# A linear-attention and feed-forward block on one core: K sums in two fp16 parts, a moved projection, a later load and another order in the first tile

## What is computed

```
q, k, v = heads(xn @ Wq), heads(xn @ Wk), heads(xn @ Wv)     # 16 heads of 64
q, k = elu(q) + 1, elu(k) + 1
k_sum = k.sum(over rows)
z = einsum(q, k_sum) + 1e-6
kv = einsum("bhnd,bhne->bhde", k, v)
out = (q @ kv / z) @ Wo + bo                                  # x = x + out
h = square(relu(xn2 @ W_fc.T));  y = h @ W_proj.T
x = x + (count of spikes of y over 5 steps) / 5
```

## Time and profile before

| what | value |
|---|---|
| median of 3 runs | 1036.33 us (1036.07 to 1036.6) |
| profiled execution, its own time | 1036.43 us |
| its span | 1034.6 us |
| PE busy | 1026.2 us |
| DVE, ACT, POOL busy | 873.8, 737.3, 654.7 us |
| TensorE clock granted | 1.00 of full speed |

### The profile page before, as it was taken

One profiled execution on the slowest core, in us unless ns is written; L12 is line 12 of the kernel. 1 busy time (PEld: TensorE's weight loads), 2 busy tenths in 40 slices (PEclk: granted clock), 3 DMA queues, 4 the chain that ended last, 5 costly groups with the idle time before them and its releaser, 6 DMA issues.

```text
span 1034.6 us, 19797 instructions
## 1 busy us (share of the span) xinstructions
PE 1026.2 (99%) x6999; PEld 653.0 (63%) x6999; DVE 873.8 (84%) x1871; ACT 737.3 (71%) x1216; POOL 654.7 (63%) x410
## 2 busy tenths in 40 slices
PE   8999999999999999999999999999999999999998
PEld 4444444444444467777777767777777777777887
DVE  7899887898888699888888888888888888888875
ACT  8888677778768758676666767676767676676664
POOL 1444434455345488777778676878777777777835
PEclk9999999999999999999999999999999999999999
DMA  4546553225323545454454454455444444544441
GB/s 132 148 127 145 121 122 88 77 63 122 87 69 82 122 76 113 93 107 99 96 128 108 82 105 95 105 106 98 97 108 108 93 103 107 108 93 93 78 80 45
DMA packets 265284, 104.24 MB, mean 101 GB/s; under 512 B 219360, under 2 KB 262624, under 8 KB 265184
## 3 DMA queue, kind: packets, MB, share of 16 engines
q1 hardware_dynamic: 265040, 102.90, 44.7%
q10 hardware_dynamic: 144, 0.07, 0.0%
HBM read 33.69 MB, written 16.79 MB: 49 GB/s over the span
## 4 chain that ended last, share of the span: by engine, by line
PE 97%; DMA 1%; DVE 1%; ACT 1%; issue 0%; ACTq 0%; DVEq 0%
PE proj L619 31%; PE acc L784 16%; PE acc L820 16%; PE acc L662 15%; PE acc L759 8%; PE acc L768 4%; PE acc L761 4%; PE proj L696 1%; PE proj L684 1%; DMA xT<-xnat 1%; ACT feat L879 0%; PE acc L633 0%; PE proj L673 0%; DMA x_t<-in_L_attn_x_dram 0%; ACT feat L875 0%
## 5 line engine op out<-in xcount | busy, mean ns | idle before, releaser
L875 ACT ACTIVATE feat<-proj 128x1024 f32<-128x1024 f32 x123 | 125.7, 1022 | 193.7 <-PE proj L619 193.7
L1555 POOL TENSOR_TENSOR qT<-qT,feat 128x1024 f32<-128x1024 f32 x60 | 142.4, 2373 | 174.8 <-DVE xnat L1186 151.3
L1590 POOL TENSOR_TENSOR h<-h_f,h 128x512 f16<-128x512 f32 x128 | 148.8, 1183 | 159.2 <-ACT h L1052 159.2
L784 PE MATMUL acc<-xn2T,wfcT 128*128 128x256 f16 x1536 | 178.0, 273 | 0.0
L820 PE MATMUL acc<-wpT,h 128*128 128x256 f16 (+1 forms) x1560 | 177.9, 271 | 0.1
L662 PE MATMUL acc<-feat,xnat 128*128 128x512 f16 x768 | 176.2, 379 | 0.0
L619 PE MATMUL proj<-wk,xT 128*128 128x512 f16 x756 | 173.3, 379 | 0.7 <-DMA xT<-xnat 0.4
L784 PEld LDWEIGHTS acc<-xn2T,wfcT 128*128 128x128 f16 x1536 | 150.3, 98 | 28.9
L1561 POOL TENSOR_TENSOR feat<-feat,rz 128x1024 f32<-128x1024 f32 x60 | 165.8, 2764 | 2.8 <-DVE rz L1293 2.8
L619 PE MATMUL proj<-wq,xT 128*128 128x512 f16 x720 | 165.2, 379 | 0.0
L820 PEld LDWEIGHTS acc<-wpT,h 128*128 128x128 f16 x1560 | 150.6, 98 | 22.7 <-issue 0.3
(11 more groups left out here) (106 smaller groups left out, 1317.9 us busy)
## 6 DMA issues: line engine op xcount, KB each, us to landing
x_t<-in_L_attn_x_dram SPq DMA_DIRECT2D x128, 128.0 KB, 2.3
xT_spill<-xT SPq DMA_DIRECT2D x64, 128.0 KB, 2.0
out_dram<-out_t SPq DMA_DIRECT2D x63, 128.0 KB, 2.1
xT<-xT_spill SPq DMA_DIRECT2D x60, 128.0 KB, 2.3
ks_all<-ks_rows SPq DMA_DIRECT2D x4, 512.0 KB, 4.5
qT<-feat SPq DMA_TRANSPOSE x120, 3.1
m_all<-in_L_attn_Wk_dram SPq DMA_DIRECT2D x4, 256.0 KB, 4.3
xT<-xnat SPq DMA_TRANSPOSE x64, 2.4
```

The costliest lines, as they stand in the source:

```text
L784: mm = pe.matmul(acc[:, 2 + g % 2, f % 2 * 2 * P:(f % 2 + 1) * 2 * P], wfcT[:, left, f * C2 + c2, :], xn2T[:, pair % 4, right * C2 + c2, : ...
L1555: pool.tensor_tensor(kacc[:, b % 2, :], kacc[:, b % 2, :], k_feat(n), ALU.add).then_inc(k_added, 1)
L1590: pool.tensor_tensor(lo, h_f[:, k % 4, :], hi, ALU.subtract).then_inc(h_lo, 1)
```

## The change

Four things. The K sums of batches 0 to 2 are split into fp16 parts, high by ACT (`ks_hi_part`, two rounds ahead of kv) and low by DVE (`ks_lo_part`, one round ahead), both scaled by 1/16, into slot 3 of `qT`; `ks_job` then runs eight fp16 matmuls of 256 columns instead of four in fp32. The two M guests of batch 2 go from rounds 54 and 56 of the K stage to steps 15 and 18 of `LATE`. `load_ks` comes one round later. `first_k_tile` completes one half of the columns before it begins the other. The order of `JOBS`, by which semaphores count, follows.

```diff
+        ks16 = qT[:, 3, :, :].rearrange("p (h k) n -> p h (k n)", h=2)
+        ones16 = sb("ones16", [P, 32], F16)
...
-        JOBS = [job for b in range(B) for job in in_order(b)]
+        JOBS = [("kv", 0, 0), *m_jobs(0), ("kv", 1, 0), *m_jobs(1), ("kv", 2, 0), ("kv", 3, 0), *m_jobs(2), *m_jobs(3)]
...
-                  52: ("kv", 2, 0), 54: ("m", 2, 0), 56: ("m", 2, 1)}
+                  52: ("kv", 2, 0)}
...
-        LATE = {7: ("kv", B - 1, 0), 26: ("m", B - 1, 0), 29: ("m", B - 1, 1)}
+        LATE = {7: ("kv", B - 1, 0), 15: ("m", 2, 0), 18: ("m", 2, 1), 26: ("m", B - 1, 0), 29: ("m", B - 1, 1)}
...
+                if n == 3:
+                    sp.wait_ge(ks_full, B - 1)
...
-                if n - 5 in GUESTS and GUESTS[n - 5][0] == "kv":
-                    load_ks(GUESTS[n - 5][1])
+                if n - 6 in GUESTS and GUESTS[n - 6][0] == "kv":
+                    load_ks(GUESTS[n - 6][1])
...
-                for right, lefts, ready in ((HI, (HI, LO), w_hi), (LO, (HI,), w_split)):
-                    for half in range(2):
-                        cols = slice(half * HALF, (half + 1) * HALF)
+                for half in range(2):
+                    cols = slice(half * HALF, (half + 1) * HALF)
+                    for right, lefts, ready in ((HI, (HI, LO), w_hi), (LO, (HI,), w_split)):
...
-                        if right == LO:
-                            mm.then_inc(k_proj if half else k_half_proj, 1)
+                    mm.then_inc(k_proj if half else k_half_proj, 1)
...
+                if b < B - 1:
+                    pe.wait_ge(ks_lo, b + 1)
+                    groups = ks16.rearrange("p h (j a r) -> p h a j r", a=4, r=32)
+                    for part in (HI, LO):
+                        for a in range(4):
+                            mm = pe.matmul(ks_bank(b)[32 * a:32 * a + 32, :], ones16[:, :], groups[:, part, a],
+                                           start=(part == HI), stop=(part == LO), skip_group_check=True)
...
+            def ks_hi_part(b):
+                act.wait_ge(k_added, BT * (b + 1))
+                wait_past(act, ks_full, b)
+                act.activation(ks16[:, HI, :], kacc[:, b % 2, :], ACT.Copy, scale=KS_SHARE).then_inc(ks_hi, 1)
...
+                if n + 2 in GUESTS and GUESTS[n + 2][0] == "kv":
+                    ks_hi_part(GUESTS[n + 2][1])
...
+            def ks_lo_part(b):
+                dve.wait_ge(ks_hi, b + 1)
+                dve.scalar_tensor_tensor(out=ks16[:, LO, :], in0=kacc[:, b % 2, :], scalar=KS_SHARE,
+                                         in1=ks16[:, HI, :], op0=ALU.mult, op1=ALU.subtract).then_inc(ks_lo, 1)
...
+            dve.memset(ones16[:, :], 1.0 / KS_SHARE).then_inc(consts_ready, 1)
...
                 if n and live(n) and n - 1 not in GUESTS and not border(n):
                     k_elu_tile(n)
+                if n + 1 in GUESTS and GUESTS[n + 1][0] == "kv":
+                    ks_lo_part(GUESTS[n + 1][1])
```

More of the change, by code:

```diff
@@ L28 @@
 M_SCALE = 64.0
+KS_SHARE = 1.0 / 16.0
 def spike_thresholds(beta=0.9, threshold=1.0, steps=5):
@@ L167, in build @@
         g_copied = [sem("g_copied_act"), sem("g_copied_dve")]
+        ks_hi, ks_lo = sem("ks_hi"), sem("ks_lo")
         ks_full, ks_turned, ks_taken = sem("ks_full"), sem("ks_turned"), sem("ks_taken")
@@ L278, in build, with m_jobs @@
         M_JOBS = 2
-        def in_order(b):
-            return [("kv", b, 0)] + [("m", b, i) for i in range(M_JOBS)]
-        JOBS = [job for b in range(B) for job in in_order(b)]
+        def m_jobs(b):
+            return [("m", b, i) for i in range(M_JOBS)]
+        JOBS = [("kv", 0, 0), *m_jobs(0), ("kv", 1, 0), *m_jobs(1), ("kv", 2, 0), ("kv", 3, 0), *m_jobs(2), *m_jobs(3)]
         GUESTS = {20: ("kv", 0, 0), 22: ("m", 0, 0), 24: ("m", 0, 1), 27: ("q", 0), 33: ("q", 1),
                   36: ("kv", 1, 0), 38: ("m", 1, 0), 40: ("m", 1, 1), 44: ("q", 2), 49: ("q", 3),
-                  52: ("kv", 2, 0), 54: ("m", 2, 0), 56: ("m", 2, 1)}
+                  52: ("kv", 2, 0)}
         Q_GUESTS = {guest[1]: n for n, guest in GUESTS.items() if guest[0] == "q"}
@@ L667, in ks_job @@
             def ks_job(b):
[L670 to L674, removed]
+                if b < B - 1:
[5 more added lines that the diff above has]
+                                           start=(part == HI), stop=(part == LO), skip_group_check=True)
+                else:
+                    pe.wait_ge(k_added, BT * (b + 1))
+                    groups = kacc[:, b % 2, :].rearrange("p (j a r) -> p a j r", a=4, r=32)
+                    for a in range(4):
+                        mm = pe.matmul(ks_bank(b)[32 * a:32 * a + 32, :], ones[:, 0:32], groups[:, a],
+                                       start=True, stop=True)
                 mm.then_inc(ks_full, 1)
@@ L714, in guest_job @@
                     m_job(*which)
-            pe.wait_ge(consts_ready, 3)
+            pe.wait_ge(consts_ready, 4)
             pe.wait_ge(xa_loaded[0], 16)
@@ L1297, in _ @@
             dve.memset(ones[:, :], 1.0).then_inc(consts_ready, 1)
-            dve.wait_ge(consts_ready, 3)
+            dve.memset(ones16[:, :], 1.0 / KS_SHARE).then_inc(consts_ready, 1)
+            dve.wait_ge(consts_ready, 4)
             stats_a(0)
```

## The result

| what | before | after |
|---|---|---|
| median us (range) of 15 executions each | 1036.34 (1035.98 to 1036.92) | 1038.66 (1038.21 to 1039.32) |
| span of the profiled execution | 1034.6 | 1036.8 |
| TensorE clock granted | 1.00 | 1.00 |

The change makes the kernel 0.22% slower: ratio 1.0022, 95% interval 1.0014 to 1.0030. The forecast was 1038.7 us, in a range of 1035.2 to 1039.8.

What follows compares the result with a forecast made beforehand. The prediction took TensorE's matmul stream as the bound (busy 1026.2 of 1034.6 us). Its terms, -0.5 - 0.9 + 0 - 0.35 + 1.75 + 0.9 + 0.9 + 0.6, gave +2.4, so 1038.7 us, range 1035.2 to 1039.8.

Steps and rivals of the forecast that it cites:

- The block: Batch 0, round 19: ks_lo waits for POOL's running K sum addition, k_lo(19) comes late, PE starts g(19) +1.75 us.
- The start: First K tile: half 0 done sooner, ACT's steps start about 0.5 us earlier, two PE gaps go: -0.5 us.
- Batches 1 and 2: The same ks_lo delay at g(35) and g(51), with wider margins and no weight split: +0.9 us each.
- K sums: Between G and kv: eight overlapping fp16 matmuls take about 0.3 us, saving 0.3 in each of three batches: -0.9 us.
- M: Batch 2's M bursts moved late: 1.09 us in either place, so work moves and nothing is saved: 0.
- The load: load_ks(2) issued one round later, behind the transpose of xT(60), so k_tile(60) loses its wait: -0.35 us.
- Rounds 54 to 58: End of K stage: rounds shrink without M, DVE falls behind beside POOL, the transpose for k_tile(58) is late: +0.6 us.
- The alternation: Rounds 54 to 58: k_lo and xn_lo each wait for one POOL piece, DVE's round some 5.7 us against 5.18.
- Rival 1: Rounds 54 to 58 are covered and the three stalls a little short: +1.5, 1037.8 us; chance 0.24.
- Rival 2: ks_lo isn't blocked by POOL; only batch 0 stalls, 0.75 us, by k_tile(21): -0.8, 1035.5 us; chance 0.14.
- Rival 3: DVE and ACT margins hide everything, matmul savings reach their ends: -2.25, 1034.1 us; chance 0.09.
- Rival 4: The fp16 sums run one after the other, +0.3 instead of -0.3 per batch: +4.2, 1040.5 us; chance 0.05.

Runs made afterwards that it cites:

- lo_first: The changed kernel with ks_lo moved ahead of k_elu on DVE, right behind xn_lo; 1035.24 us, ratio 0.9991.
- hi_only: The changed kernel without ks_lo, the K sums of batches 0 to 2 adding the high parts alone, ks_hi kept; 1035.19 us, ratio 0.9988.
- sums_fp32: The changed kernel with the K sums of all batches in fp32 again, the other three parts kept; 1035.32 us, ratio 0.9992.
- m_late_only: The kernel before with M of batch 2 as late guests alone; 1036.60 us, ratio 1.0001.
- pool_waits: The changed kernel with POOL's K sum additions of rounds 18, 34 and 50 waiting until ks_lo is done; 1038.74 us, ratio 1.0024.

## Why the prediction came out right

**The block.** This step carried the sign, and it held in its details: `ks_lo` 2.52 us long in all three batches (forecast about 2.5), ending 1.08 after the addition (1.1), the wait in batch 0 +1.71 (+1.75). The semaphore, for which no run had shown the 0.1 us allowed, took 0.06 (117.00 to 117.06). The price was read from a pair of smaller instructions late in the kernel; what carried over was the rule that they show, that the one issued second waits for the other's end. Its other half, that POOL pays when `ks_lo` is issued first, held in lo_first. So the sign turned on `ks_lo` being issued 0.92 us behind the addition, since `k_elu` stood ahead of it.

**The start.** -0.49 for -0.5, and for the reason given: ACT began its step on the first half, idle until 11.38 before, without a wait.

```profile
10.89 0.58 ACT L888 ACTIVATE feat<-acc 128x512 f32<-128x512 f32 x1
```

**Batches 1 and 2.** +0.81 each against +0.9, within the reading of start times. Batch 1 has `k_tile(40)` besides, +0.22. It waits for `k_elu(39)`, behind the kv guest of round 36 and the M guest of round 38, and lo_first doesn't have it, so it comes from where `ks_lo` stands too. The step that the kv guest gives the helpers enough time to catch up was therefore slightly wrong: DVE still carried some of the delay past both guests.

**K sums.** Mis-sized: 0.23 each, not 0.3. The estimate of 0.22 us for eight fp16 matmuls took the overlap to be four-fold; they take 0.33 from start to start (119.75 to 120.08), and four take 0.22 (hi_only).

**M.** 0 in the sum, -0.20 measured, which was the lower bound. A burst takes 1.12 us in the late stage and 1.22 in the K stage; the difference lies between its start and that of the next tile (1.03 and 1.13 us), and no run says why. The row's 1.09 us, which the forecast compared, is the same in both places.

**The load.** -0.52 against -0.35. The prediction took the idle bracket of 0.36 and forgot the tail of 0.16 that it had added for `k_tile(3)` further up. The price of 0.52 is that of this one execution of before; others lost 0.14 to 0.63 there.

**Rounds 54 to 58.** Half the size, +0.33 for +0.6, and at `k_tile(58)` only. The alternation is as forecast: a piece of POOL in front of `k_lo` and of `xn_lo` in turn. In the timeline of DVE in after, `k_lo` takes 1.69 and `xn_lo` 1.26 us, for 1.22 and 0.42 without:

```profile
325.51 1.69 DVE L1255 TENSOR_TENSOR feat<-feat 128x1024 f16<-128x1024 f32 x1
327.11 1.26 DVE L1206 TENSOR_TENSOR xnat<-xn,xnat 128x256 f16<-128x256 f32 x1
```

But sums_fp32 and m_late_only, which have M late and no split, show the very same pair without a wait of PE:

```profile
322.86 1.69 DVE L1253 TENSOR_TENSOR feat<-feat 128x1024 f16<-128x1024 f32 x1
324.47 1.26 DVE L1204 TENSOR_TENSOR xnat<-xn,xnat 128x256 f16<-128x256 f32 x1
```

These are sums_fp32's. Its `xn_lo` ends at 325.73, and PE starts `k_tile(58)` at 328.29, 2.56 later; m_late_only has 2.56 too (326.16 and 328.72). In after `xn_lo` ends at 328.37, and PE could have gone on at 330.70, 2.33 later, which no longer covers the transpose. So the alternation was forecast well and is hidden by itself; the wait comes from DVE standing 0.23 us later against PE. The cheaper K sums, by which PE comes 0.23 us earlier, don't explain that: lo_first and hi_only have them and M late as well, and their margins are 2.55 us (325.04 to 327.59 and 325.08 to 327.63), without a wait. What after has besides is the late `k_lo(51)` of round 52, and its DVE then runs longer beside POOL at `k_lo(54)`, one tile ahead of the pair above:

```profile
319.77 0.85 DVE L1195 TENSOR_SCALAR xn<-x_t,mv,newt 128x256 f32<-128x256 f32 x1
320.54 2.06 DVE L1255 TENSOR_TENSOR feat<-feat 128x1024 f16<-128x1024 f32 x1
```

In lo_first the same two take 0.40 and 1.58. pool_waits, whose `k_lo(51)` is late too, has the 2.33 again (328.50 to 330.83) and loses 0.17 there. So this term comes from where `ks_lo` stands, together with M's absence; the forecast had derived it from M's absence alone.

**The sum.** +2.4 forecast, +2.15 by start times, +2.32 by the medians. Terms that came out dearer than forecast: K sums 0.21, `k_tile(40)` 0.22, the first tile's landing 0.13, together 0.56. Cheaper: rounds 54 to 58 0.27, M 0.20, the load 0.17, the three waits at G 0.04 + 0.09 + 0.09, together 0.86. That the total came this close is partly luck, since errors of both signs cancelled; what isn't luck is that the three waits make 3.33 of it, forecast 3.55.

**The rivals.** Rival 1, with rounds 54 to 58 free and the stalls short, isn't told from the forecast by time alone: its +1.5 lies at the lower end of the interval. By rows it was about as near: rounds 54 to 58 cost 0.33, midway between its 0 and the forecast's 0.6, and the three stalls 3.33, between its 3.2 and 3.55. What brought the total to the forecast were `k_tile(40)` and the first tile's landing, +0.35, which neither had. Rival 2 (`ks_lo` not blocked) fell in after and is what lo_first makes true: 1035.24 against its 1035.5. Rival 3 set its turning point at `k_lo(19)` ending by 115.7; it ended at 117.00, and fell. Rival 4, serial sums, fell: 0.33 us for eight against 0.86.

## What to carry to other kernels

When an instruction with two SBUF inputs is added to DVE, look for the POOL instruction that starts near it and ask which is issued first: the same instruction in another place of the same round was worth 3.4 us here, five times what the cheaper K sums gave (0.69). Holding POOL back didn't remove the block here, it gave it to the next DVE instruction that the addition holds up; moving the short instruction ahead of the long one did. And price every wait by start times, not by its idle bracket: each bracket in the K stage lacked some 0.16 us of the tail in front of it.

## What the runs showed of the hardware

- A tensor_scalar of 128x256 fp32 with one tensor input in SBUF is held up by a POOL tensor_tensor in full: 1.64 us instead of 0.38, ending 0.15 after it. A scalar_tensor_tensor of 1024 columns with one fp32 and one fp16 input in SBUF is as well (2.52 for 1.22), and one with an input in PSUM isn't (`k_elu`, 1.22 beside the addition).
- The block works both ways and by issue: POOL's addition takes 3.21 us when it is issued 0.22 behind `ks_lo`, 2.36 alone.
- Small pieces of both engines alternate: `k_lo` and `xn_lo` of rounds with two POOL pieces take 1.69 and 1.26 us for 1.22 and 0.42 alone, and the POOL piece that goes between them takes 2.02 for 1.09.
- Four fp16 matmuls of 256 columns into four groups of 32 output partitions take 0.22 us together, eight take 0.33. By 2.59 / 12 / 2 = 0.108 each that is two and three matmuls' time: they overlap, though four don't cost one.
- The first tile's start spread over 0.59 us (9.10 to 9.69) from profile to profile, in seven kernels with the same code ahead of it. A change of 0.5 us at the start is seen only relative to the first tile.
